# Down products of the shared FFN groups as three fp32r products

## The reference

```
def ffn(x):                       # x: (4096, 128), E = 8 experts, top 2, 2 shared groups of width 128
    logits = x @ gate_w.T
    scores = softmax(logits);  w, idx = top_k(scores, 2);  w = w / (w.sum + 1e-20)
    pos = running count of each expert's tokens;  w = w * (pos < capacity)
    comb[n, e] = w where chosen, else 0
    y  = sum_e comb[n, e] * (silu(x @ we_gate[e].T) * (x @ we_up[e].T)) @ we_down[e].T
    sh = (silu(x @ ws_gate.T) * (x @ ws_up.T)) @ ws_down.T
    return y + sh

x = x + 0.5 * ffn(layernorm(x))
x = x + attention(layernorm(x))   # 16 heads of 64, rotary and Fourier terms on q and k, softmax
x = x + 0.5 * ffn(layernorm(x))
```

## Time and profile before

| what | us |
|---|---|
| runs before | 1268.78, 1264.79, 1268.65 (median 1268.65) |
| the profiled execution | 1265.84, its span 1264.0 |
| first FFN, about | 0 to 237 |
| attention, about | 237 to 1064 |
| second FFN, about | 1064 to 1264 |
| busy in the span | TensorE 1224.8, VectorE 958.6, GpSimd 897.0, ScalarE 629.8 |
| granted clock of TensorE | 0.999 of full speed |

### The profile page before, as it was taken

How to read it: one execution, slowest core, us unless ns; L and a number is a source line. 1 busy time by engine, 2 the same in 40 slices (tenths; PEclk the granted TensorE clock), 3 DMA queues, 4 the chain that set the end, 5 groups by cost and what they waited for, 6 DMA issues and landing times.

```text
span 1264.0 us, 20948 instructions
## 1 busy us (share of the span) xinstructions
PE 1224.8 (97%) x7346; PEld 777.6 (62%) x7346; DVE 958.6 (76%) x1439; ACT 629.8 (50%) x921; POOL 897.0 (71%) x652
## 2 busy tenths in 40 slices
PE   5999999899999999999999999999999999999998
PEld 3666666456666656565666666665666655666665
DVE  6666687778898888888888888788888766666632
ACT  3444532455555555546555555555555554434422
POOL 0444346688898999898889889889989862543443
PEclk9999999999999999999999999999999999999999
DMA  5351241123232323233332323232323221442140
GB/s 170 135 184 55 81 145 24 34 52 69 57 72 52 77 52 74 54 69 60 64 66 60 68 60 69 52 77 54 73 54 73 56 44 20 142 143 105 47 159 17
DMA packets 118677, 95.35 MB, mean 75 GB/s; under 512 B 75760, under 2 KB 85008, under 8 KB 118320
## 3 DMA queue, kind: packets, MB, share of 16 engines
q1 hardware_dynamic: 118064, 93.75, 30.0%
q10 hardware_dynamic: 512, 0.26, 0.1%
HBM read 57.53 MB, written 2.88 MB: 48 GB/s over the span
## 4 chain that ended last, share of the span: by engine, by line
PE 85%; DVE 6%; issue 4%; ACT 2%; POOL 2%; DMA 1%; SPq 0%; ACTq 0%; DVEq 0%; POOLq 0%
PE banks L1165 17%; PE banks L1144 14%; PE banks L455 12%; PE banks L468 8%; PE banks L1083 7%; PE banks L1003 6%; PE banks L1181 5%; PE banks L1149 4%; PE banks L1190 4%; PE banks L1011 3%; PE banks L1122 1%; DVE side_turned L702 1%; PE banks L410 1%; POOL work L1438 1%; PE banks L417 1%
## 5 line engine op out<-in xcount | busy, mean ns | idle before, releaser
L1015 DVE TENSOR_REDUCE neg_max<-banks 128x2 f32<-128x1024 f32 x256 | 305.3, 1226 | 12.7 <-PE banks L1003 7.7
L1267 ACT ACTIVATE work<-banks 128x1024 f32<-128x1024 f32 x256 | 262.5, 1027 | 92.7 <-PE banks L1149 76.6
L1165 PE MATMUL banks<-work 128*64 128x512 f32 x1024 | 233.8, 598 | 0.0
L1438 POOL TENSOR_TENSOR work<-work 128x1024 f32<-128x1024 f32 x64 | 158.8, 2482 | 74.2 <-PE banks L1165 74.2
L1428 POOL TENSOR_TENSOR turn<-turn,side_turned 128x512 f32<-128x512 f32 x128 | 164.9, 1311 | 30.7 <-DMA side_turned<-side 30.7
L1422 POOL TENSOR_TENSOR turn<-turn,fenc 128x512 f32<-128x512 f32 x128 | 163.3, 1298 | 2.0 <-DVE side L1338 2.0
L1433 POOL TENSOR_TENSOR qk_l<-turn,qk_h 128x512 fp32r<-128x512 f32 x128 | 162.1, 1289 | 2.1 <-ACT qk_h L992 2.1
L1165 PEld LDWEIGHTS banks<-work 128*64 128x64 f32 x1024 | 67.8, 136 | 132.7 <-issue 110.0
L1359 DVE TENSOR_TENSOR work<-work 128x1024 f32<-128x1024 f32 x64 | 107.4, 1677 | 37.7 <-PE banks L1165 37.5
L816 POOL TENSOR_TENSOR o_raw<-o_raw,work 128x512 f32<-128x512 f32 x52 | 67.2, 1293 | 88.0 <-DVE o_raw L734 80.7
L816 POOL TENSOR_TENSOR work<-work 128x512 f32<-128x512 f32 x44 | 56.6, 1297 | 96.0 <-DVE work L734 49.6
(11 more groups left out here) (178 smaller groups left out, 2454.7 us busy)
## 6 DMA issues: line engine op xcount, KB each, us to landing
work<-share SPq DMA_DIRECT2D x32, 1024.0 KB, 9.4
side_turned<-side SPq DMA_DIRECT2D x256, 128.0 KB, 3.1
rec_all<-rec_d SPq DMA_DIRECT2D x128, 128.0 KB, 2.9
x_tok<-in_x SPq DMA_DIRECT2D x8, 256.0 KB, 6.3
out<-x_tok SPq DMA_DIRECT2D x8, 256.0 KB, 9.4
work<-in_w_gate_up SPq DMA_DIRECT2D x1, 1280.0 KB, 6.7
work<-in_w_qk SPq DMA_DIRECT2D x1, 1024.0 KB, 11.8
den_d<-den_rows ACTq DMA_DIRECT2D x64, 4.0 KB
```

The lines of the kernel that those rows point to most:

```text
L1015: return nc.vector.tensor_reduce(neg_max[:, g % 2, qt::DH], of, AX.X, ALU.max, negate=True)
L1165: ins = nc.tensor.matmul(o_bank(g)[OWN[h], :], v_all[:, kt, n * DH:(n + 1) * DH], pt[:, g % 2, kt, h * T:(h + 1) * T], start=(kt == 0), st ...
L1267: nc.scalar.activation(pt[:, g % 2, kt, :], S[kt].rearrange("p h q -> p (h q)"), ACT.Exp, scale=QSCALE).then_inc(s["probs"], 1)
L1438: nc.gpsimd.tensor_tensor(pt[:, g % 2, 2, :], pt[:, g % 2, 2, :], pt[:, g % 2, 3, :], ALU.add).then_inc(s["second_sum"], 1)
```

## The change

From the third batch on, a shared unit's down product becomes three fp32r products: high weight by high hidden, low weight by high hidden, high weight by low hidden. The parts are made as follows.

- `hid_high(i)` on ScalarE copies the hidden tile of unit i into fp32r, in period i + 1 behind silu(i + 1). The tile is `shift[:, g]`, a buffer of the attention.
- `hid_low(i)` on GpSimd subtracts, at unit i's place in its stream, into `qk_h[:, 2, g]`, also the attention's.
- down(i) waits for `hid_low`.
- `down_high` and the subtraction to `down_lo` split the weights of both shared groups once, in period 9 of f1, on ScalarE and VectorE.
- The attention's copy into set 2 of `qk_h` waits until f1's last shared down product is done.

The twelve units are 20, 21, 30, 31, ..., 70, 71, in both FFNs. Units of the first two batches and the experts stay as they were.

```
+DOWN_SPLIT_AT = 9
...
+        down_hi = sb("down_hi", [P, NSH, D], F32R)
+        down_lo = sb("down_lo", [P, NSH, D], F32R)
...
+        hid_lo = qk_h[:, 2]
...
+        hid_hi = shift
...
+            def split(i):
+                if i >= N:
+                    return False
+                b, g = UNITS[i]
+                return b >= CB and g < NSH
...
                 def down(i):
                     b, g = UNITS[i]
-                    if g < NSH:
+                    if split(i):
+                        pe.wait_ge(s["hid_low"], splits(i + 1))
+                        pe.wait_ge(down_lo_ready, 1)
+                    elif g < NSH:
                         pe.wait_ge(s["gated"], i + 1)
...
-                    nc.tensor.matmul(Y[b % 2], down_w[:, g, :], hid(i), start=(i == first_of(b)),
-                                     stop=(i == last_of(b))).then_inc(s["down"], 1)
+                    parts = ((down_w, hid(i)),)
+                    if split(i):
+                        parts = ((down_hi, hid_hi[:, g]), (down_lo, hid_hi[:, g]), (down_hi, hid_lo[:, g]))
+                    for m, (w, h) in enumerate(parts):
+                        ins = nc.tensor.matmul(Y[b % 2], w[:, g, :], h, start=(i == first_of(b) and m == 0),
+                                               stop=(i == last_of(b)))
+                    ins.then_inc(s["down"], 1)
...
+                def hid_high(i):
+                    b, g = UNITS[i]
+                    act.wait_ge(s["gated"], i + 1)
+                    if splits(i) >= NSH:
+                        act.wait_ge(s["down"], first_of(b - 1) + g + 1)
+                    nc.scalar.activation(hid_hi[:, g], hid(i), ACT.Copy).then_inc(s["hid_high"], 1)
+
+                def down_high():
+                    act.wait_ge(in_down, 16)
+                    nc.scalar.activation(down_hi[:], down_w[:, 0:NSH], ACT.Copy).then_inc(down_hi_ready, 1)
...
                     if i < N:
                         silu(i)
+                    if 0 < i and split(i - 1):
+                        hid_high(i - 1)
                     c, q = chunk(i)
+                    if not last and i == DOWN_SPLIT_AT:
+                        down_high()
...
                     if i < N:
                         gated(i)
                     c, q = chunk(i)
+                    if not last and i == DOWN_SPLIT_AT:
+                        dve.wait_ge(down_hi_ready, 1)
+                        tt(down_lo[:], down_w[:, 0:NSH], down_hi[:], ALU.subtract).then_inc(down_lo_ready, 1)
...
+                def hid_low(i):
+                    pool.wait_ge(s["hid_high"], splits(i + 1))
+                    nc.gpsimd.tensor_tensor(hid_lo[:, UNITS[i][1]], hid(i), hid_hi[:, UNITS[i][1]],
+                                            ALU.subtract).then_inc(s["hid_low"], 1)
+
                 for i in range(N):
                     if UNITS[i][1] >= NSH:
                         weighted(i)
+                    elif split(i):
+                        hid_low(i)
...
             def high(act, g, part):
                 act.wait_ge(s["k_sum" if part == K else "q_sum"], g + 1)
+                if g == 1 and part == K:
+                    act.wait_ge(ffn1["s"]["down"], ffn1["units"] - E)
```

More of the change, by code:

```diff
@@ L187, in macaron @@
         w_hi_ready, w_lo_ready = sem("w_hi_ready"), sem("w_lo_ready")
+        down_hi_ready, down_lo_ready = sem("down_hi_ready"), sem("down_lo_ready")
         fenc_ps, fenc_ready = sem("fenc_ps"), sem("fenc_ready")
@@ L322, in ffn @@
                 "normed", "xn_ready", "xn_first", "xt_ps", "x_hi_ready", "x_lo_ready", "logits_t", "logits_copied", "logits", "shifted", "exps", "masks", "pos",
-                "routed", "turned", "rows_ready", "gate_ps", "up_ps", "silu", "weighted", "gated", "down", "y_copied", "yt_ps", "x_done")}
+                "routed", "turned", "rows_ready", "gate_ps", "up_ps", "silu", "weighted", "gated", "hid_high", "hid_low", "down", "y_copied", "yt_ps", "x_done")}
             listed = tuple(sem(f"{tag}_listed{c}") for c in range(CHUNKS))
@@ L362, in experts, with splits @@
                 return sum(1 for b, g in UNITS[0:i] if g >= NSH)
+            def split(i):
[3 more added lines that the diff above has]
+                return b >= CB and g < NSH
+            def splits(i):
+                return sum(1 for n in range(i) if split(n))
             def last_of(b):
```

## The result

| | us |
|---|---|
| before, 4 runs | median 1267.41 (1264.79 to 1268.78) |
| after, 4 runs | median 1283.83 (1283.74, 1283.91, 1287.68, 1280.07) |
| ratio | 1.0132, 95% interval 1.0097 to 1.0168 |
| difference | +16.7 (12.3 to 21.3) |
| profiled executions | 1265.84 and 1283.74, spans 1264.0 and 1281.9: +17.9 |

The account below looks back on a forecast made before the run. It took TensorE, busy for 97% of the span, as the bound, with VectorE's chain setting the time at eight places. Terms -4.0 + 6.1 + 9.0 + 1.1 + 0.7 = +12.9 us gave 1280 us, range 1268 to 1288.

Parts of the forecast that it names:

- TensorE's gain: Shared groups' down products: three split products take 0.70 us instead of 0.87, 0.165 us gained each, 24 times, -4.0 us.
- four norm places: Waits before an odd batch's token transposes, after the layer norm: a low part blocks VectorE, 1.5 us each, +6.1 us.
- four route places: Waits for the expert masks: two low parts on GpSimd each block a VectorE instruction, 2.25 us each, +9.0 us.
- end of the first FFN: Unit 70's low part delays the attention's first rotation, then the copy of y and TensorE's transposes: +1.1 us.
- weights split: The one-time subtraction to down_lo on VectorE waits for GpSimd and delays the logits product: +0.7 us, between 0 and 1.3.
- The 0.33 us that I had put into each wait: At each norm and route place TensorE arrives 0.33 us earlier through two cheaper down products, so its wait grows by that.
- the 1.9 that I had named as a sign: Sign that the forecast is right: TensorE's wait before the odd batch's transposes near 1.9 us at four places.
- about 1.2 us each: Sign that the forecast is right: VectorE's L696 and L698 in the route places take about 1.2 us each.
- Rival 2: At the route places L698 slips in before the second low part: 1.0 instead of 2.25 us each, about 1274; chance 0.20.
- Rival 1: The gain lands whole, with under about 4 us lost to all waits together: about 1263; chance 0.07.
- rival 4: The three split products start no closer than today's pair and save nothing: about 1281.5; chance 0.05.
- rival 3: VectorE meets one more GpSimd instruction at eight places (+10), or longer waits end the first FFN: about 1289; chance 0.10.

Follow-up runs that it names:

- e4: The full change without GpSimd's low parts, the third product reading the high part again: 1266.01 against 1266.94 us for the kernel before, ratio 0.9993.
- e2: The full change with products split only for the shared units of batches 3 and 5, where the routing runs: 1277.43 against 1266.94 us for the kernel before.
- e10: The full change with the low parts on VectorE, one period later, instead of GpSimd: 1274.01 against 1267.15 us for the kernel before, ratio 1.0053.
- e6: The full change with nine unread products on TensorE at each of four mask waits: 1277.59 against 1266.33 us for the kernel before, ratio 1.0092.
- e5: The full change with its parts made and waited for, but the down product left as one fp32 product: 1283.21 against 1266.33 us for the kernel before.
- e9: The kernel before plus a ScalarE copy and GpSimd subtraction of constant tiles at the same 24 places, result unread: 1283.97 against 1267.15 us without them.
- e7: The full change with everything behind the layer norm one period later in the second and third chunk: 1275.48 against 1266.33 us for the kernel before.
- e1: The full change with products split only for the shared units of batches 2 and 4, ahead of the norm places: 1273.47 against 1266.94 us for the kernel before.
- e8: The kernel before with everything behind the layer norm one period later in the second and third chunk: 1267.12 us, ratio 1.0006 to the kernel before.
- e12: The kernel before with everything behind the norm one period later, and positions and shares one more: 1265.95 us, ratio 0.9990 to the kernel before.

## Why the prediction was nearly right, and what it missed

The sign, the place and the mechanism held; the time lies in the range. That it does owes something to the range's width: 8 us above the forecast left room for a term of 6.4 that the sum did not have. Term by term, from the profiled execution, the waits read from start to start:

| term | forecast | measured |
|---|---|---|
| TensorE's gain, 24 products | -4.0 | -4.0 (0.70 us each) |
| four norm places | +6.1 | +6.4 |
| four route places | +9.0 | +8.2 |
| end of the first FFN | +1.1 | +0.9 |
| weights split | +0.7 | 0 |
| TensorE's clock | not in the sum | +6.4 |
| the wait for `comb_w` near 167 us | not in the sum | -0.7 |
| sum | +12.9 | +17.2, of 17.9 |

- *TensorE's gain*: right in each step. The experiments add what it is worth alone: -0.9 us (e4), not -4.0, because VectorE ends last at the eight places. The 0.33 us that I had put into each wait is that.
- *Norm place*: 1.6 us a place for 1.5. The chain moved by 1.3 where I had 1.2, and the gain of two cheaper products is swallowed on top, as priced. What I had not seen is where TensorE pays: it stops for the up bank first, at 87.21, then at the even batch's transposes, and is itself later at the odd batch's, so the wait at L425 is 1.0 and not the 1.9 that I had named as a sign. The sum of the stops is that of the one.
- *Route place*: both blocks and their sizes are right (1.07 and 1.22 for "about 1.2 us each"; 2.05 more wait a place for 2.25). Rival 2 had only the second block missing; it did not come.
- *Weights split*: I had GpSimd first; VectorE was. The lower bound of 0 held. It hangs on tenths of a microsecond: in e2 and e10 GpSimd was first, and the same VectorE instruction took 1.48 and 1.25 us instead of 0.42.
- *The missing step*: the sum priced the waits as idle time alone. I took TensorE's clock for full since the trace of before shows it full in both FFNs; but the longest waits that it has there are 1.2 us (at 33.52) and 1.35 (at 1086.93), so that trace could not speak for waits of 2.3. The one lower window that it has is its last, 0.74 at 1260 us. (In the attention it waits 1.73 us once, at 242.19, and stays full.) With 1.6 us a fall, and four falls in the profiled execution, that is 6.4 us, and e6 takes about 5 of them away. The difference between forecast and result, 3.8 us of the medians, is this term less what the route places, the end of the first FFN, the weights and `comb_w` gave less than forecast.
- Rival 1 and rival 4 are out by the rows, and so is rival 3: no place met a further GpSimd instruction (the one that holds L740 at 108.71 for 1.35 us held L702 at 105.58 before). The result came near rival 3's side of the forecast by another mechanism than its own.

Open: 0.7 us between the sum and the profiled pair, of which about 0.5 come in during the attention; and what decides whether the clock falls behind a given wait. The spread of the changed kernel, 1280 to 1288 us with clocks of 0.997 to 0.993, would fit with more or fewer falls, but these were counted in one execution of each kernel.

## What to carry to other kernels

An idle engine is not a free one: before moving elementwise work to GpSimd, read what VectorE does in that very microsecond, and whether TensorE waits for it soon after; a 1.3 us instruction there turned small ones of 0.2 us into 1.1 to 1.3, and the same work on the busy VectorE was 10 us cheaper. What a wait costs is read from start to start and not from the idle time in brackets, which came 2.3 us short over the four norm places. A gain on the busiest engine is worth only what the engines that end last at its waits let through (here 0.9 of 4.0 us). A forecast that makes TensorE wait longer than anywhere in the trace should carry the clock's fall behind the wait in its range, as a term of its own.

## What was not expected of the hardware

- Behind waits of 1.8 to 2.6 us TensorE's granted clock fell to its 1.2 GHz level for about 3.4 us, which costs 1.6 to 1.7, but not always. It happened behind four of four mask waits in the changed kernel and in e5, three of four in e9, two of four in e2 and in e7. Over all traces that were kept, but for e1's, 28 waits in the FFNs last 1.75 us or longer, and the clock fell behind 19. None is seen behind the mask waits of 1.1 to 1.5 us of e8 and e10, none behind the 1.7 us that every kernel waits once at the start of the attention, and none where unread products filled the wait (e6). A shorter wait doesn't exclude it: behind the 1.2 us near 33 us it fell in e2, e9, e10 and e12, and neither in the kernel before nor after the change.
- Which of VectorE and GpSimd gives way is a matter of tenths of a microsecond. At 78.63 and 78.68 GpSimd was first and VectorE lost 1.1 us; in e10, at 108.65 and 108.87, VectorE was first and GpSimd lost 0.3.
- GpSimd running back to back let exactly one small VectorE instruction through between two of its own, at the four route places of the changed kernel and of e9 alike, so two low parts cost two blocks of about 1 us.
